# Sharing the row maxima of a softmax between three engines: seven quarter tiles in place of two half tiles

## The reference

```python
qkv = einsum('btd,de->bte', x, w_qkv) + b_qkv
q, k = rope(q), rope(k)
attn = softmax(einsum('bhqd,bhkd->bhqk', q, k) / sqrt(16))
x = layernorm(x + einsum('bte,ef->btf', attn @ v, w_out) + b_out)
h = silu(x @ w_gate.T / 127) * (x @ w_up.T / 127)
x = layernorm(x + h @ w_down.T / 127)
```

## Time and profile before

| | |
|---|---|
| median of 3 runs | 2852.1 us (2850.74 to 2855.02) |
| profiled execution, its own time | 2853.19 us |
| its span, first to last instruction | 2851.1 us |
| mean granted TensorE clock | 0.989 |
| TensorE matmul busy | 2820.5 us, 99% |
| VectorE busy | 2691.3 us, 94% |
| ScalarE busy | 2578.5 us, 90% |
| GpSimd busy | 1416.2 us, 50% |

### The profile page before, as it was taken

The page is one execution under the profiler, slowest core; times in us unless marked ns, Lnnn a source line. Parts: engine busy times, 40 slices in busy tenths (PEclk is TensorE's granted clock), DMA queues, the critical chain, the costliest instruction groups (busy, mean ns, idle before and its releaser), DMA issues. The chain is left out here.

```text
span 2851.1 us, 70512 instructions
## 1 busy us (share of the span) xinstructions
PE 2820.5 (99%) x27022; PEld 882.6 (31%) x27022; DVE 2691.3 (94%) x3088; ACT 2578.5 (90%) x4778; POOL 1416.2 (50%) x4133
## 2 busy tenths in 40 slices
PE   8989999999999999999999999999999999999998
PEld 4531222222222222222222222222222222246665
DVE  7989999999999999999999999999999999947777
ACT  5756999999999999999999999999999999975655
POOL 7851444444444444444444444444444444436553
PEclk9978999999999999999999999999999999999999
DMA  5431111111111111111111111111111111233431
GB/s 196 141 119 27 37 35 36 35 36 35 36 35 36 35 36 35 35 35 36 35 36 35 36 36 35 36 35 36 36 36 35 35 36 35 70 93 89 119 97 38
DMA packets 121519, 146.56 MB, mean 51 GB/s; under 512 B 52832, under 2 KB 87520, under 8 KB 121180
## 3 DMA queue, kind: packets, MB, share of 16 engines
q1 hardware_dynamic: 120892, 142.02, 17.3%
q10 hardware_dynamic: 288, 0.01, 0.0%
HBM read 106.30 MB, written 35.13 MB: 50 GB/s over the span
## 5 line engine op out<-in xcount | busy, mean ns | idle before, releaser
L102 DVE TENSOR_REDUCE tile_max<-s_ps 128x1 f32<-128x1024 f32 (+1 forms) x2048 | 2273.9, 1181 | 4.3 <-PE s_ps L91 2.5
L1076 ACT ACTIVATE probs<-bank_ps 128x512 f32<-128x512 f32 x4096 | 2188.9, 603 | 67.0 <-PE bank_ps L956 40.5
L966 PE MATMUL bank_ps<-probs,kept_v 128*17 128x256 f32 x16384 | 1283.2, 385 | 0.0
L91 PE MATMUL s_ps<-k,q 64*128 64x512 f16 x4096 | 1267.0, 387 | 11.1 <-DVE tile_max L102 9.3
L956 PE MATMUL bank_ps<-q,k 64*128 64x512 f16 x4096 | 1252.5, 382 | 1.2 <-ACT probs L1076 0.8
L1211 POOL TENSOR_TENSOR larger<-spared 128x256 f32<-128x256 f32 x1107 | 342.8, 310 | 659.3 <-ACT spared L1051 582.3
L956 PEld LDWEIGHTS bank_ps<-q,k 64*128 64x128 f16 x4096 | 271.9, 93 | 910.7 <-ACT probs L1076 823.7
L966 PEld LDWEIGHTS bank_ps<-probs,kept_v 128*17 128x17 f32 x16384 | 271.8, 95 | 806.4 <-ACT probs L1076 412.1
L1220 POOL TENSOR_TENSOR spared<-spared,larger 128x256 f32<-128x256 f32 x984 | 318.0, 323 | 81.9
L1213 POOL TENSOR_SCALAR larger<-larger 128x256 f32<-128x256 f32 x1107 | 261.4, 236 | 96.8
L91 PEld LDWEIGHTS s_ps<-k,q 64*128 64x128 f16 x4096 | 259.5, 94 | 50.4 <-DVE tile_max L102 46.5
(11 more groups left out here) (119 smaller groups left out, 1625.2 us busy)
## 6 DMA issues: line engine op xcount, KB each, us to landing
q<-q_parts SPq DMA_DIRECT2D x193, 128.0 KB
k<-k_parts SPq DMA_DIRECT2D x193, 128.0 KB
x_t<-in_x_t SPq DMA_DIRECT2D x16, 512.0 KB, 7.6
q_parts<-parts SPq DMA_DIRECT2D x32, 256.0 KB, 2.6
k_parts<-parts SPq DMA_DIRECT2D x32, 256.0 KB, 2.6
heads_out<-sums SPq DMA_DIRECT2D x256, 32.0 KB, 2.0
kept_v<-heads_out SPq DMA_DIRECT2D x16, 512.0 KB, 5.9
kept_v<-inverses_out SPq DMA_DIRECT2D x32, 256.0 KB
```

Of the source, the lines that this page charges most:

```text
L91: mm = pe.matmul(s["s_ps"][g % 2][:, j * BANK:(j + 1) * BANK], s["q"][h % 2][rows, r // KW * P:(r // KW + 1) * P], s["k"][h % 2][rows, at: ...
L102: dve.tensor_reduce(s["tile_max"][h % 2][:, r // KW, r % KW:r % KW + 1], s["s_ps"][g % 2][:, columns], AX.X, ALU.max).then_inc(s["s_read"], 1)
L966: mm = pe.matmul(o_ps[h][c * 32:c * 32 + VM, at:at + HALF], t["kept"][:, h, kt, :], probs[(h * KT + kt) % RING][:, c * BANK + at:c * BANK ...
L1076: act.activation(probs[(h * KT + kt) % RING][:, c * BANK:(c + 1) * BANK], st_ps[n][:, :], ACT.Exp, scale=scale).then_inc(exp_done, 1)
```

## The change

Seven tiles of a head, tiles 0, 3, 6, 9 and 17, 20, 23, in two batches, give up their first 256 columns each (QUARTER). ScalarE copies them (`keep_quarter`) one even exponential earlier than before in relation to the tile: behind exponential 2n and in front of 2n + 1, whose slot n + 1 holds the tile. VectorE waits for the copy (`quarter_kept`) and then reduces the other 768 columns; TensorE's wait for the copy goes. GpSimd folds a batch at once, in eight levels over four or three tiles. The last level has two instructions in place of one, since the rows of `tile_max` are not all neighbours. `spared` has two buffers, so a copy waits for the batch before last. TURN goes from 2 to 4: VectorE's transpose of the joined maxima stands behind tile 4 of the next head. The last head has no second batch, and a memset gives its unused entries the lowest value.

```diff
-    ROWS = (2, 20)
+    BATCHES = ((0, 3, 6, 9), (17, 20, 23))
+    MOST = max(len(rows) for rows in BATCHES)
+    QUARTER = BANK // 2
     INVERT = 10
-    TURN = 2
+    TURN = 4
...
-    SPARED = [h * MAXES + r for h in range(2, HEADS) for r in ROWS][:-1]
-    LEVELS = 9
-    FOLDS = 3 * LEVELS
+    SPARES = [[h * MAXES + r for r in rows] for h in range(2, HEADS) for rows in BATCHES][:-1]
+    SPARED = [g for batch in SPARES for g in batch]
+    LEVELS = 8
+    RUNS = 2
+    FOLDS = 3 * LEVELS + RUNS - 1
...
                 if j == 0:
                     wait(pe, s_read, g - 1)
-                    if g - 2 in SPARED:
-                        pe.wait_ge(half_kept, SPARED.index(g - 2) + 1)
...
+            def keep_quarter(batch, i):
+
+                g = SPARES[batch][i]
+                act.wait_ge(half_done, SPARED.index(g) + 1)
+                wait(act, folded, FOLDS * (batch - 1))
+                act.copy(spared[batch % 2][:, i, :], s_ps[g % 2][:, 0:QUARTER]).then_inc(quarter_kept, 1)
...
-                    g = (h + 1) * MAXES + LEAD + e // 2
+                    g = (h + 1) * MAXES + LEAD + (e + 2) // 2
                     if e % 2 == 0 and g in SPARED:
-                        keep_half(SPARED.index(g))
+                        for batch, tiles in enumerate(SPARES):
+                            if g in tiles:
+                                keep_quarter(batch, tiles.index(g))
...
                 dve.wait_ge(s_done, g + 1)
-                own = slice(BANK, WIDE) if g in SPARED else slice(0, WIDE)
+                own = slice(0, WIDE)
+                if g in SPARED:
+                    dve.wait_ge(quarter_kept, SPARED.index(g) + 1)
+                    own = slice(QUARTER, WIDE)
                 tile_maximum(dve, s, g, T, own)
...
+            def larger_of(a, b, more, out, sem, step):
+
+                pool.tensor_tensor(more, b, a, ALU.subtract).then_inc(sem, 1)
+                pool.wait_ge(sem, step + 1)
+                pool.tensor_scalar(more, more, -LOWEST, 0.0, ALU.min, ALU.max).then_inc(sem, 1)
+                pool.wait_ge(sem, step + 2)
+                pool.tensor_tensor(out, a, more, ALU.add).then_inc(sem, 1)
...
+            def fold(batch):
+
+                tiles = SPARES[batch]
+                h, n, wide = tiles[0] // MAXES, len(tiles), QUARTER // 2
+                pool.wait_ge(quarter_kept, SPARED.index(tiles[-1]) + 1)
+                held = spared[batch % 2]
+                for k in range(LEVELS - 1):
+                    step = FOLDS * batch + 3 * k
+                    wait(pool, folded, step)
+                    larger_of(held[:, 0:n, 0:wide], held[:, 0:n, wide:2 * wide], larger[:, 0:n, 0:wide],
+                              held[:, 0:n, 0:wide], folded, step)
                     wide //= 2
...
+                for at, end in zip(starts, starts[1:] + [n]):
+                    pool.tensor_tensor(tile_max[h % 2][:, rows[at]:rows[end - 1] + 1, KW:KW + 1], held[:, at:end, 0:1],
+                                       larger[:, at:end, 0:1], ALU.add).then_inc(folded, 1)
```

More of the change, by code:

```diff
@@ L820, in attend @@
         max_scaled = sb("max_scaled", [P, 32])
-        spared = sb("spared", [P, BANK])
-        larger = sb("larger", [P, BANK // 2])
+        spared = [sb(f"spared{i}", [P, MOST, QUARTER]) for i in range(2)]
+        larger = sb("larger", [P, MOST, QUARTER // 2])
         more_top = sb("more_top", [P, QT])
@@ L841, in attend @@
         half_done = sem("half_done")
-        half_kept = sem("half_kept")
+        quarter_kept = sem("quarter_kept")
         folded = sem("folded")
+        lowered = sem("lowered")
         head_max = sem("head_max")
@@ L1187, in join @@
                 pool.wait_ge(s_read, (h + 1) * MAXES)
-                wait(pool, folded, FOLDS * sum(g < (h + 1) * MAXES for g in SPARED))
+                wait(pool, folded, FOLDS * sum(batch[0] < (h + 1) * MAXES for batch in SPARES))
                 wait(pool, max_turned, h - 1)
+                if h == HEADS - 1:
+                    pool.wait_ge(lowered, 1)
+                step = JOINS * h
+                wait(pool, head_max, step)
                 joined = head_top[i][:, 0:QT]
[L1191 to L1208, removed]
-                    wait(pool, folded, step)
[L1210 to L1220, removed]
-                    wide //= 2
+                larger_of(tile_max[i][:, :, 0], tile_max[i][:, :, 1], more_top[:, :], joined, head_max, step)
@@ new lines, in join @@
+                pool.wait_ge(head_max, step + 3)
+                larger_of(joined, tile_max[i][:, :, KW], more_top[:, :], joined, head_max, step + 3)
+            def fold(batch):
[5 more added lines that the diff above has]
+                    step = FOLDS * batch + 3 * k
+                    wait(pool, folded, step)
+                    larger_of(held[:, 0:n, 0:wide], held[:, 0:n, wide:2 * wide], larger[:, 0:n, 0:wide],
+                              held[:, 0:n, 0:wide], folded, step)
+                    wide //= 2
+                step = FOLDS * batch + 3 * (LEVELS - 1)
+                more = larger[:, 0:n, 0:1]
+                pool.wait_ge(folded, step)
+                pool.tensor_tensor(more, held[:, 0:n, 1:2], held[:, 0:n, 0:1], ALU.subtract).then_inc(folded, 1)
+                pool.wait_ge(folded, step + 1)
+                pool.tensor_scalar(more, more, -LOWEST, 0.0, ALU.min, ALU.max).then_inc(folded, 1)
+                pool.wait_ge(folded, step + 2)
+                wait(pool, head_max, JOINS * (h - 1))
+                rows = [g % MAXES // KW for g in tiles]
+                starts = [i for i in range(n) if i == 0 or rows[i] != rows[i - 1] + 1]
+                for at, end in zip(starts, starts[1:] + [n]):
+                    pool.tensor_tensor(tile_max[h % 2][:, rows[at]:rows[end - 1] + 1, KW:KW + 1], held[:, at:end, 0:1],
+                                       larger[:, at:end, 0:1], ALU.add).then_inc(folded, 1)
@@ L1238, in _ @@
                 cut(h)
-                for n in range(len(SPARED)):
-                    if SPARED[n] // MAXES == h + 1:
-                        fold(n)
+                if h == HEADS - 3:
+                    unspared = slice(BATCHES[-1][0] // KW, QT)
+                    pool.wait_ge(head_max, JOINS * (h + 1))
+                    pool.memset(tile_max[(HEADS - 1) % 2][:, unspared, KW:KW + 1], LOWEST).then_inc(lowered, 1)
+                for batch, tiles in enumerate(SPARES):
+                    if tiles[0] // MAXES == h + 1:
+                        fold(batch)
                 if h == HEADS - 2:
```

## The result

The changed kernel takes 2918.5 us, the median of five runs (2913.8 to 2923.1), beside 2852.1 (2850.7 to 2855.0), also of five runs, before: a ratio of 1.0231, with an interval of 1.0216 to 1.0246. It is slower by 66 us. The profiled execution is itself the median: 2918.52 us, with a span of 2916.7 us and a granted clock of 0.987.

What follows compares the result with a forecast made beforehand. TensorE's floor of 35.01 us a head was taken as the bound, with VectorE's lag and long ScalarE copies adding 0.66. Stalls of 62 x 1.1 = 68 us less 13 gained gave +55: 2906 us, range 2860 to 2944.

Steps and rivals of the forecast that it cites:

- The turn: Transpose moved behind tile 4: a 5.3 us chain with 5.0 us of room stalls TensorE 0.4 us at tile 10.
- Rival 2: The chain stays hidden before tile 10's transposed matmul and VectorE's relief shows: -13 us, 2839; chance 0.08.
- The packets: TensorE's 16 KB instruction packets lengthen the chain of the maxima in 6 heads in 10, by 1.2 us each.
- 1.8 if all: Mean stall per head at tile 10, in us, if every head's chain met an instruction packet; 1.1 was the estimate.
- Rival 1: The chain stalls at tile 10 but packets don't lengthen it: 62 x 0.4 - 13 = +12 us, 2864; chance 0.2.
- VectorE: 768-column reductions take 0.864 us instead of 1.131; a head's 34.7 us falls under TensorE's floor, 0.05 charged for lag.
- ScalarE: Seven 256-column copies replace two of 512; step 0.25 us, 0.21 free, 0.04 each, six counted: 0.25 us a head.
- The drain's 0.13: ScalarE's copy of the sums delays TensorE by 0.13 us in each head.
- 13 us over 62 heads: Gain without the stall: a head of 35.45 us (35.01 + 0.05 + 0.25 + 0.13), 0.21 less than before.
- GpSimd: Batch folds take 11.9 us for four tiles and 10.7 for three; the join ends near tile 3.2 of the next head.
- Rival 3: A copy costs near its upper bound, or the three-tile fold exceeds 13 us: 2943 at a 0.35 step; chance 0.1.

Runs made afterwards that it cites:

- experiment 2: The changed kernel with VectorE's transpose back behind tile 2 (TURN = 2 instead of 4): 2861.8 us, ratio 1.0034 to the kernel before.
- experiment 4: The changed kernel with 78 small matmuls (156 TensorE instructions) added before the first head's transposed scores, shifting TensorE's instruction packets: 2887.3 us, ratio 1.0119.
- experiment 5: The changed kernel with TURN = 2, without the seven copies, VectorE's wait for them and the folds; maxima omit 256 columns per tile: 2824.9 us.
- experiment 9: The changed kernel with LEAD = 12 instead of 10, transposed matmuls two tiles further behind the scores: 2870.3 us, ratio 1.0057.
- experiment 8: The changed kernel with eleven 128-column copies, TURN = 2, second batch one tile later, TensorE's q and k wait one matmul earlier: 2824.2 us.

## Why the prediction was right

The forecast was slower by 55 us, and it is 66. The mechanism was the one named, and the steps came out so:

- **The turn.** The transpose was put 0.72 us into tile 5's slot; in the trace it stands at tile 5.66 on average, which is the same place. The chain is 5.28 us long in the 11 heads without a packet, where 5.3 was worked out. The pair of tile 10 is 0.54 us apart in these heads, a stall of 0.32 over the 0.22 of an undisturbed pair, for 0.4 worked out; half of it is there without a stall too (0.38 in experiment 2). Rival 2, which wanted 0.4 us more room, fell.
- **The packets, where luck helped.** The forecast was 6 heads in 10 at 1.2 us each, 0.7 in the mean (its "1.8 if all" should be 1.6 by that number). In the trace a 16 KB packet lies beside the chain's transfers in 46 of 62 heads, more than was thought, and lengthens the chain by only 0.85 us in the mean; 5 more heads have an 8 KB packet alone, at 0.54, which the sum did not have. These errors cancel: 0.67 us. The chain's mean is 5.95 us where 5.3 + 0.7 = 6.0 was worked out. The slow drift is as predicted: 16 KB packets meet the chain in heads 17 to 46 before, and in heads 16 to 62 after. Rival 1 (2864), without packets, is not what experiment 4 shows (2887): of the 23 us between, some 9 lie in tile 10, by the 8 KB packets, and the rest beside the stall. The stall as a whole was put at 68 us; by experiment 2 it is 57.
- **VectorE.** A 768-column tile takes a step of 0.86 to 0.91 us (0.864 estimated), and the relief is real: with the turn at tile 2 a head lasts 35.80 us, and that is made up without any lag of VectorE: 35.01, five copies of 0.074 and tile 1's of 0.045, 0.14 for the drain, 0.06 in tiles 31 and 0, 0.164 in tile 10, together 35.79. The 0.05 us charged for a lag of eight long tiles was not needed.
- **ScalarE, the term that was mis-sized.** "A copy costs 0.25 - 0.21 = 0.04 (0.02 to 0.26); six count". It costs 0.074: the copy starts 0.457 us into the slot and not 0.42, and its step is 0.269 and not 0.25. The gap had only 0.21 us, so an error of 0.03 us nearly doubled the excess. Seven copies are 0.5 us a head, not 0.25. The drain's 0.13 was right (0.14).
- **What the sum had no term for.** Tiles 31 and 0 cost 0.06 us more (by my reading two waits that are worked off in a row), and tile 10's slot, with no stall at all, still lasts 1.258 in experiment 2: its copy, and 0.09 more where the copy meets the three waits in front of the matmul. With these waits and no copy the slot lasts 1.103 (experiment 5), with the copy and the waits two tiles further on 1.167 (experiment 9). With the copies this is why "13 us over 62 heads" of gain became a loss of 10.
- **GpSimd.** The 512-element level takes 1.27 us and the 384 one 1.0; the batch of three takes 10.4 us (10.7 predicted) and ends far from anybody's wait. Rival 3 fell in both of its halves, but its first half pointed the right way: 0.03 us of a copy's step and start are 13 us of the run.

So two errors met: measured by experiment 2, the stall was 11 us too large and everything beside it 23 us too small. That they partly cancel is luck too. The Trainium skill, VectorE: DVE Perf Modes, section on the TRN2 errata, gives a ScalarE instruction from PSUM 172 cycles plus its columns at 1.2 GHz, an estimate of 0.36 us for 256 columns. In this trace the step is 0.27 and 0.37 is how long the copy lasts; for the time until the next instruction the measurement decides.

## What to carry to other kernels

Before a step of a dependent chain is moved, write the chain's length beside the room it has, part by part from the trace: this one had 2.2 us to spare, and two tiles of 1.1 us used them up, in a kernel whose busy shares looked as before. A piece of work that is slipped between two others is free or not by whether it fits its gap: eleven copies of 0.16 us in a gap of 0.2 cost nothing where seven of 0.27 cost 7 x 0.074 x 62 = 32 us. Judge relief of one engine by what its receiver has left at that very place, and take a chain of small transfers with the slowest landing seen in any stretch, not with the median of a calm one.

## What the runs showed of the hardware

- Packets of instructions delay small dependent transfers. With TensorE's (16 KB) the 16 KB write lands after 2.2 instead of 1.4 us, the 4 KB reads after 2.7 instead of 2.0 (medians of stretches). The 8 KB packets do it too: 2.0 us for the write. TensorE's can be moved by adding instructions elsewhere, and in a loop whose count is near a multiple of the packet's they stay in the same place for tens of heads (16 to 62 in the changed kernel). The Trainium skill, Runtime: NRT & Kernel Launch, section Instruction fetch mechanics, calls the cost of going on to the next block mostly hidden. TensorE's own stream agrees with it: with three packets a head, each of the slots of tiles 15 to 31 keeps its own length from head to head to 0.01 us. The chain of transfers does not, and here that was about 31 us.
- ScalarE's copies from PSUM hold up the next instruction for less than they last: 0.466, 0.269 and 0.162 us for 512, 256 and 128 columns, which last 0.592, 0.372 and 0.266.
- A wait that had long been met was free on TensorE by itself, but where two or three stood in a row and the first was met late, the slot was 0.06 to 0.09 us longer. For tile 10 the slots of 1.258, 1.103 and 1.167 us above show it; for tile 31 experiment 8 took one away and its slot came to 1.10 us, with the batch moved at the same time.
